# First linear layer closed by one maximum with the negated bias, the rest of the bias sent once through the next layer's weights

## What is computed

```python
h = relu(einsum('ts,bsh->bth', adj, x @ Wg0 + bg0))
h = relu(einsum('ts,bsh->bth', adj, h @ Wg1 + bg1))
for p in range(1, 5):                      # windows of p nodes
    last = lstm_last(Wih[p-1], Whh[p-1], ...)   # p steps, gates i f g o
    h[:, idx_p, :] = last
x = layernorm(x + h)
x = layernorm(x + gnn2(x, adj, ...))       # A_hat, W1, batch norm, relu, W2, batch norm
```

## Time and profile before

| | us |
|---|---|
| median of 3 runs (883.23 to 884.33) | 883.76 |
| profiled execution, its own time | 883.75 |
| its span, first to last instruction | 881.9 |
| TensorE busy | 845.5 |
| VectorE busy | 710.4 |
| ScalarE busy | 595.4 |
| one period in the loop | 90.2 |

### The profile page before, as it was taken

The page is one execution under the profiler, slowest core; times in us unless marked ns, Lnnn a source line. Parts: engine busy times, 40 slices in busy tenths (PEclk is TensorE's granted clock), DMA queues, the critical chain, the costliest instruction groups (busy, mean ns, idle before and its releaser), DMA issues.

```text
span 881.9 us, 15645 instructions
## 1 busy us (share of the span) xinstructions
PE 845.5 (96%) x5048; PEld 535.0 (61%) x5048; DVE 710.4 (81%) x1794; ACT 595.4 (68%) x1186; POOL 67.9 (8%) x58
## 2 busy tenths in 40 slices
PE   8999999999999999999999999999999988899984
PEld 5666667666666667666767675766665655333442
DVE  5577878887888879888987888888888977577995
ACT  4576666766676667766776767676767644792398
POOL 0000000000000000000000000000000000000575
PEclk9999999999999999999999999999999989999998
DMA  6000010012001100110010101010000001144145
GB/s 207 25 25 1 8 65 1 29 44 74 1 25 48 67 4 24 48 39 33 24 48 24 48 24 48 25 49 25 25 25 26 25 34 63 56 139 139 71 168 190
DMA packets 17692, 44.96 MB, mean 51 GB/s; under 512 B 2032, under 2 KB 3184, under 8 KB 17520
## 3 DMA queue, kind: packets, MB, share of 16 engines
q1 hardware_dynamic: 17648, 44.39, 14.1%
HBM read 27.61 MB, written 16.78 MB: 50 GB/s over the span
## 4 chain that ended last, share of the span: by engine, by line
PE 76%; issue 9%; DVE 8%; ACT 4%; DMA 1%; SPq 1%; POOL 0%; ACTq 0%; DVEq 0%; POOLq 0%
PE gate_bank L761 30%; PE gate_bank L737 9%; PE gate_bank L753 6%; PE gate_bank L754 5%; PE gate_bank L792 5%; PE front_bank L664 3%; PE back_bank L710 3%; PE front_bank L681 3%; PE front_bank L675 3%; DVE bn L974 3%; PE front_bank L669 3%; PE back_bank L718 1%; ACT z L893 1%; PE back_bank L720 1%; PE back_bank L719 1%
## 5 line engine op out<-in xcount | busy, mean ns | idle before, releaser
L761 PE MATMUL gate_bank<-h_hi,w_hi 128*128 128x256 f16 (+3 forms) x592 | 175.9, 315 | 5.9 <-DVE h_lo L1068 3.4
L844 ACT ACTIVATE gate_i<-gate_bank,lstm_bias 128x256 f32<-128x256 f32 (+2 forms) x176 | 99.9, 568 | 115.0 <-PE gate_bank L792 87.5
L761 PE MATMUL gate_bank<-h_hi,w_lo 128*128 128x256 f16 (+3 forms) x592 | 175.7, 314 | 0.0
L761 PE MATMUL gate_bank<-h_lo,w_hi 128*128 128x256 f16 (+3 forms) x592 | 175.5, 314 | 0.0
L844 ACT ACTIVATE gate_o<-gate_bank,lstm_bias 128x512 f32<-128x512 f32 (+2 forms) x176 | 99.6, 570 | 37.0 <-PE gate_bank L792 28.1
L753 PE MATMUL gate_bank<-s_hi,w_hi 128*128 128x256 f16 (+2 forms) x384 | 112.9, 302 | 0.8 <-DVE s_hi L1065 0.8
L1051 DVE SCALAR_TENSOR_TENSOR gate_f<-gate_o,gate_f 128x512 f32<-128x512 f32 (+2 forms) x176 | 94.0, 539 | 23.9 <-ACT gate_f L850 22.4
L754 PE MATMUL gate_bank<-s_hi,w_lo 128*128 128x256 f16 (+2 forms) x384 | 112.6, 302 | 0.0
L844 ACT ACTIVATE gate_g<-gate_bank,lstm_bias 128x256 f32<-128x256 f32 (+2 forms) x176 | 99.5, 566 | 7.7 <-PE gate_bank L737 3.7
L792 PE MATMUL gate_bank<-s_lo,w_hi 128*128 128x256 f16 (+2 forms) x384 | 100.3, 302 | 0.0
L850 ACT ACTIVATE gate_f<-cell 128x512 f32<-128x512 f32 (+2 forms) x176 | 87.9, 507 | 9.7 <-DVE cell L1042 5.5
(11 more groups left out here) (159 smaller groups left out, 1512.0 us busy)
## 6 DMA issues: line engine op xcount, KB each, us to landing
x_front<-in_x SPq DMA_DIRECT2D x16, 512.0 KB, 4.1
rows_sb<-in_x SPq DMA_DIRECT2D x16, 512.0 KB, 3.3
x_kept<-normed_sb SPq DMA_DIRECT2D x16, 512.0 KB, 2.7
z<-x_kept SPq DMA_DIRECT2D x16, 512.0 KB, 3.7
out<-z SPq DMA_DIRECT2D x15, 512.0 KB, 3.1
z<-in_wr SPq DMA_DIRECT2D x1, 1536.0 KB, 6.9
out<-z SPq DMA_DIRECT2D x2, 256.0 KB, 2.2
wih_sb<-in_wih SPq DMA_DIRECT2D x1, 192.0 KB, 2.6
```

Source lines behind the costliest of these rows:

```text
L761: last = mm(like(to[:, at:at + size], view), w, view, start=start and j == 0, stop=stop and j + 1 == len(views), skip_group_check=shared)
L844: ins = activation(acts[gate][h][:, 0:n], gate_bank[h][bank_of(job, gate)][:, 0:n], ACT.Tanh if gate == "g" else ACT.Sigmoid, bias=lstm_bi ...
```

## The change

The ReLU of the first layer is rewritten: relu(y + b) = max(y, -b) + b. VectorE takes the maximum of the product and a tile `neg_bias0` and writes `h0T`, and ScalarE does nothing there. The b that is left passes through the next layer: (max + b) w1 = max w1 + b w1, where b w1 is once computed on TensorE in the first half, ahead of its first lin1 product, and added to `bias1` on VectorE ahead of the first half's lin1 output. The negation is one operation in the setup. Numbers of the setup semaphores shift accordingly, and the signals "biased" of lin0 become its "out". The planner's table loses the ReLU and its offset of -0.05.

```diff
-            if stage == "lin0":
-                ops.append(("DVE", (stage, "biased", n), vector_us(BANK), after))
-                after = [(stage, "biased", n)]
-            ops.append(("DVE", (stage, "out", n), vector_us(BANK), after) if stage == "lin1" else
-                       ("ACT", (stage, "out", n), scalar_us(BANK, 0) + (0.04 if stage == "lin0" else 0), after))
-            bank_free = (stage, "biased" if stage == "lin0" else "out", n)
+            ops.append(("DVE", (stage, "out", n), vector_us(BANK), after) if stage in ("lin0", "lin1") else
+                       ("ACT", (stage, "out", n), scalar_us(BANK, 0), after))
+            bank_free = (stage, "out", n)
...
-AHEAD_KIND = {("ACT", "mix0", "out"): 0.75, ("ACT", "lin0", "out"): -0.05, ("ACT", "lstm", 3): 0.05,
+AHEAD_KIND = {("ACT", "mix0", "out"): 0.75, ("ACT", "lstm", 3): 0.05,
...
+                if op == ("lin1", "product", 0, 0) and isinstance(g, int) and (g, h) == (0, 0):
+                    pe.wait_ge(sem_degree, 5)
+                    mm(setup_bank[:, 0:P], bias0[:], w1_sb[:], start=True, stop=True).then_inc(sem_setup_pe, 1)
...
                 if op == ("mix1", "product", 1, 3) and isinstance(g, int) and (g, h) == (0, 0):
                     pe.wait_ge(sem_setup, 2)
+                    pe.wait_ge(sem_degree, 7)
...
                     if n == 1 and alone:
-                        wait(pe, ("lin0", "biased", 0), g, h)
+                        wait(pe, ("lin0", "out", 0), g, h)
...
-                    elif stage == "lin0":
-                        wait(act, (stage, "biased", n), g, h)
-                        ins = activation(h0T[:, n, :], h0T[:, n, :], ACT.Relu)
...
             dve.wait_ge(sem_degree, 5)
+            ve.tensor_scalar(neg_bias0[:], bias0[:], -1.0, None, ALU.mult).then_inc(sem_degree, 1)
+            dve.wait_ge(sem_degree, 6)
...
-                    dst, bias = (h0T, bias0) if stage == "lin0" else (mixed, bias1)
+                    if op == ("lin1", "out", 0) and isinstance(g, int) and (g, h) == (0, 0):
+                        dve.wait_ge(sem_setup_pe, 2)
+                        ve.tensor_tensor(bias1[:], bias1[:], setup_bank[:, 0:P], ALU.add).then_inc(sem_degree, 1)
+                        dve.wait_ge(sem_degree, 7)
+
+                    dst, bias, how = (h0T, neg_bias0, ALU.max) if stage == "lin0" else (mixed, bias1, ALU.add)
                     signal(ve.tensor_tensor(dst[:, n, :].rearrange("p (b n) -> p b n", n=P),
-                                            front_to(g, h, n)[:].rearrange("p (b n) -> p b n", n=P), over4(bias), ALU.add),
+                                            front_to(g, h, n)[:].rearrange("p (b n) -> p b n", n=P), over4(bias), how),
                            op, h)
```

More of the change, by code:

```diff
@@ L189, in signal_of @@
         return "front_product"
-    return "front_biased" if what == "biased" or op[0] == "lin1" else "front_out"
+    return "front_biased" if op[0] in ("lin0", "lin1") else "front_out"
 def count_signals():
@@ L320, in gnn_lstm_kernel @@
         bias0 = sb("bias0", [P, P])
+        neg_bias0 = sb("neg_bias0", [P, P])
         bias1 = sb("bias1", [P, P])
@@ L673, in front_product @@
                         if alone:
-                            wait(pe, ("lin0", "biased", 1) if n == 0 else ("lin1", "out", 0), g, h)
+                            wait(pe, ("lin0", "out", 1) if n == 0 else ("lin1", "out", 0), g, h)
                     ins = mm(cols, flat(h0T[:])[:, b * P:(b + 1) * P], w1_sb[:], start=True, stop=True)
@@ L943, in prepare_back @@
                 ve.tensor_scalar(w_hi[:], w_stage, W_SCALE, None, ALU.mult).then_inc(sem_degree, 1)
-                dve.wait_ge(sem_degree, 6)
+                dve.wait_ge(sem_degree, 8)
                 for s in range(3):
@@ L949, in prepare_back @@
                 ve.tensor_scalar(gw1_hi[:], gw1_stage, W_SCALE, None, ALU.mult).then_inc(sem_degree, 1)
-                dve.wait_ge(sem_degree, 7)
+                dve.wait_ge(sem_degree, 9)
                 ve.scalar_tensor_tensor(out=gw1_lo[:], in0=gw1_stage, scalar=W_SCALE, in1=gw1_hi[:], op0=ALU.mult,
                                         op1=ALU.subtract).then_inc(sem_split, 1)
-                dve.wait_ge(sem_setup_pe, 2)
+                dve.wait_ge(sem_setup_pe, 3)
                 ve.tensor_scalar(ahatT[:], setup_bank[:, 0:P], small[:, 3:4], A_SCALE, ALU.mult, ALU.mult).then_inc(sem_ahat, 1)
```

## The result

The kernel after takes 911.18 us (median of 4 runs, 910.18 to 914.73) against 883.67 before (median of 4): a ratio of 1.032, 95% interval 1.029 to 1.035. That is slower by 27.5 us, more than twice the 11.7 that was forecast, and 1.7 us above the upper end of the range.

A forecast was written before the change was run, and what follows sets the result against it. TensorE was taken as the bound, busy 845.5 of 881.9 us. Terms: 883.75 + 7.0 (periods) + 5.4 (end) - 0.8 (loop) = 895.4 us; own range 886 to 907, 886 to 909.5 with the slower rivals.

The forecast's parts named there:

- the setup at 0: Once-only negation, fp32 product and add near the start: between -0.7 and +1 us, taken as 0.
- Rival B: Shorter chain alone matters: TensorE regains 2.6 us of h0T waits and 0.8 of loop passes, 880.4 us; chance 0.10.
- edit (4): The planner's changed table shifts all its later greedy choices; loop has two passes, not four; carries the whole sum.
- The term of a period: +1.4: Each period of recurrent work: 0.75 + 0.75 - 0.4 + 0.3 = +1.4 us.
- The priced place: Loop, around gate_o of step 2.1: 0.75 us wait until gate_i, 0.75 more before step 3.0 until h_lo.
- place two: Front's single bank, between mix0 of n=0 and n=1: 0.15 us each, 0.3 with the sequencer's reload.
- the gain taken as 0.4: Period's wait of 0.41 us ahead of 260.56 in before, covered in after by a back product: -0.4 us.
- I count five periods: Straight periods ahead of and behind the loop share its misfit; five periods counted: +7.0 us, ends 0 and 15.
- The end: +5.4: End of the recurrent part, last half alone in more steps: 2.6 + 0.4 + 0.75 + 3.4 - 1.8 = +5.4 us, ends +2 and +12.
- a second wait above 2 us: Sign that the forecast is right: last stretch some 5 us longer, with a second wait above 2 us in it.
- The loop: -0.8: Two loop passes fewer, looped period 90.2 us against straight 89.8: -0.8 us; longer program costs nothing.
- The upper rival's 909: Slower side in full: 2.5 us a period six times, 5.4 at the end, two half-clock stretches there, 909 us; chance 0.09.

The follow-up runs named there:

- E1: New arithmetic (maximum, negated bias, bias sent through w1) with every engine's list in the order of the kernel before, ReLU struck out: 883.24 us, ratio 1.0004 to before.
- e2: Old arithmetic (add and ReLU) in the order planned for the kernel after, ReLU put back into ScalarE's list: 918.96 us, ratio 1.042 to before.
- e3: Kernel after, with each x_front load issued by ScalarE on its own queue behind its last copy of mix0: 899.03 us, ratio 1.020 to before.
- e8: On e3, in the two loop passes, gate o of step 2.1 and its activation moved behind gates of step 4.2: 902.62 us, ratio 1.0208 to before.
- e5: On e3, the last of the eight chunks put in the order of the kernel before: 893.95 us, ratio 1.0125 to before.
- e7: Kernel before, same order, with two loop passes and the other two written out: 882.73 us, ratio 0.9993 to before.
- e9: Kernel after with its offsets, but TensorE durations in the planner's table as measured in before's trace: 891.01 us, ratio 1.0079 to before.

## Why the prediction was wrong, step by step

**Right in kind.** The direction, the cause and the places. E1 and e2 show that the order is the whole of it and the arithmetic nothing: the maximum at the price of the add (taken 0.691, measured 0.691), the ReLU's relief at 0 in a period (89.81 us in either), the setup at 0 (e1's first period begins at 100.04 where before's did at 100.35). Rival B fails with this: where the order stayed, there was no gain of 2.6 us either.

**The step that failed: edit (4), "All else of the sum is here", which took the order of the four engines that the planner lays for the whole order.** It put the loads of x_front at nothing without a reason. SyncE's list is laid by nobody but the text, and the forecast let the back stage move past it without looking at what waits behind. The back stage's last z came later against the front, the load of x_front stands behind a wait for that z, and TensorE was without its input for 4.3 and 1.9 us, with the clock at half during and behind the first. e3 prices it at 12.2 us of the 27.5; its trace shows 8.8 of them in the first two periods and 0.9 in the loop, and 1.5 lie in the closing stages, which the loads don't touch. The prediction has no term for it and no rival with this mechanism.

**The term of a period: +1.4, measured +1.9 and +2.6 in the loop, +1.7 and +1.8 with timely loads (e3).** The priced place is there: 0.75 and 0.75 foreseen, 0.77 and 0.74 measured in the prediction's own distances. The rest of the term is partly luck. The 0.3 of place two doesn't show (no wait of 0.15 us or more stands there in a loop pass of after, and no run shows the sequencer's reload that it names), the gain taken as 0.4 was a wait of the weight loads and the stream had lost only 0.3 there (260.56, less the pass before it, which starts at 260.15 and takes 0.11), and a wait until rows_sb was left out (idle 0.5 and 0.2 in the two passes), where the two tokens products stand closer together than before. Places don't simply add up either: e8 removed one of the two and the pass didn't get shorter.

**"I count five periods" of the same kind.** The number came out near, the kind only in part. With the loads set right (e3) the five have 1.2, 2.1, 1.6, 1.7 and 1.8 us more without work than before, 8.4 in all against 7.0. The priced place stands in the last three. The first loses its time mainly until a gate_o (idle 1.0), the second until the maximum's output (0.9) and until z_moments (0.9), places that nobody had walked.

**The end: +5.4, measured +8.0 in the trace, 5 to 8 by e5.** The places that were priced held, in distances from pass to pass: 2.1 to 3.0 was taken at 2.6 and took 3.0; 3.0 to 3.1 at 0.4, took 0.2 (at input o of 3.1); 3.1 to 3.2 at 0.75, took 0.8; the two bare steps at 1.7 each, took 1.5 each; 3.2 to 4.0 was to shrink by 1.8 and did (3.12 to 1.29 idle). That is 5.2 of the 5.4. The rest are places that weren't walked: 1.9 us of idle time at step 4.0 of the half before the last, 1.3 and 0.9 at the last lin1, which waited for VectorE's outputs, and 1.9 instead of 0.2 ahead of the last mix, against waits of 0.8, 0.6 and 0.6 that before had and after has not. The prediction's sign for the end, "a second wait above 2 us", could not decide: before had two already, 3.12 and the tokens' 2.23, so it was not "one place" that was bare, and after has two as well, 2.82 and 2.54.

**The loop: -0.8**, measured -0.5 with an interval that includes both 0 and -0.8 (e7); the trace of e7 has 0.3 and 0.4 us less in the two periods that were written out.

**The upper rival's 909** was near the result for a wrong reason: it wanted 2.5 us in six periods and two more half-clock stretches at the end. There was one such stretch inside a period, and it came from the load; the end had no more of them than before (its mean clock is 0.98, and was 0.97). The Trainium skill's rule in "TensorE: Matmul & The Clock Gate", "What's actually happening", that activity releases the throttled default, fits it: the clock went to 0.50 in the course of the 4.3 us wait, came back with TensorE at work again, and was 1.00 throughout that period once the wait was gone (e3).

## What to carry to other kernels

Where a table of numbers lays the order, an edit to the table is an edit to every list, so try the arithmetic in the old order first (e1): it says in one run whether the idea or the shuffle is being measured. Then look at each queue that the planner doesn't lay, above all DMA issues behind another stream's waits, because the planner will move work past them blindly. An offset table fitted to one set of operations doesn't carry over to the next; here measured durations and offsets fitted anew gave 10 us with the new arithmetic and 8 with the old, more than the edit could. And when one experiment is dearer than its edit explains, look in its trace for a single place first: in e2 one stand of VectorE made 6.7 of 7.9 us.

## What the hardware showed unexpectedly

- Two input passes of 168 columns, or one of 336 read with a stride of three, go by at 0.22 us, as long as a 512-column pass and not at the 0.145 of a contiguous 336-column one. The planner's table had 0.14 to 0.15 for them. The run with TensorE's measured durations was 20 us faster (e9), part of it because no load came late in its order.
- In the course of a single wait of 4.3 us on TensorE the granted clock fell, and some 5 us behind it passed at half clock, with fp32 products of 128 columns passing in about twice the time.
- The closing stages, the same instructions in every kernel, took 131 to 133 us in the profiled executions. A difference of 1.5 us between two kernels here can lie in stretches that neither edit touches.
- In e2 VectorE stood 2.59 and 1.75 us with nothing that the profile shows it waiting for, where its loop begins the second pass; after, where VectorE has the same list, has no such stand.
